# LSTM windows laid out by step, a graph layer in groups of four samples, and a wide layer kept instead of computed twice

## The reference

```python
# L0: eight Euler steps of a graph diffusion (not touched)
# L1: spectral layer, U = eigenvectors of the normalized Laplacian (512x512)
agg = einsum('mn,bnd->bmd', U.T, h);  y = relu(agg @ W1 + b1) @ W2 + b2;  x += einsum('nm,bmd->bnd', U, y)
# L2: A_hat is 512x512, W1 widens 128 to 256, batch statistics over all 8192 rows
a = einsum('nm,bmd->bnd', A_hat, h).reshape(-1, 128)
y = relu(batchnorm(a @ W1.T + b1)) @ W2.T + b2;  x += batchnorm(y)
# L3: two graph convolutions, then for p in 1, 2, 3, 4:
wins = h[:, :nw*p, :].reshape(16*nw, p, 128)      # nw = 512 // p windows of p nodes
last = lstm(Wih[p-1], Whh[p-1], bih[p-1], bhh[p-1], wins)   # p steps, 4 gates
h[:, arange(nw)*p + p-1, :] = last                # written back in place
x += h
```

## Time and profile before

| what | value |
|---|---|
| median of 3 runs | 4364.65 us (4363.6 to 4366.91) |
| profiled execution, its time | 4359.52 us |
| profiled execution, its span | 4357.7 us |
| busy: PE, DVE, ACT, POOL | 2952.5, 2978.4, 982.9, 764.9 us |
| mean granted TensorE clock | 0.818 |

### The profile page before, as it was taken

How to read it: one execution, slowest core, us unless ns; L and a number is a source line. 1 busy time by engine, 2 the same in 40 slices (tenths; PEclk the granted TensorE clock), 3 DMA queues, 4 the chain that set the end, 5 groups by cost and what they waited for, 6 DMA issues and landing times.

```text
span 4357.7 us, 70705 instructions
## 1 busy us (share of the span) xinstructions
PE 2952.5 (68%) x21286; PEld 1968.4 (45%) x21286; DVE 2978.4 (68%) x18190; ACT 982.9 (23%) x3671; POOL 764.9 (18%) x3343
## 2 busy tenths in 40 slices
PE   2899998888888899999710011010064958699998
PEld 1677777777777765555410000000042623354433
DVE  6677888888888868888878889999822122414323
ACT  0222222322322212222210000000013121336532
POOL 0121222222222222333222221111000000000000
PEclk6789999999989959999855555555587979799998
DMA  2000000000000000000000000000000000000000
GB/s 97 2 2 2 2 2 2 2 2 2 2 2 2 2 1 2 2 2 2 1 0 0 0 0 0 0 0 0 0 0 0 0 19 0 0 0 0 1 0 39
DMA packets 3104, 21.16 MB, mean 5 GB/s; under 512 B 432, under 2 KB 560, under 8 KB 1072
## 3 DMA queue, kind: packets, MB, share of 16 engines
q1 hardware_dynamic: 2736, 16.85, 1.0%
HBM read 12.66 MB, written 4.19 MB: 4 GB/s over the span
## 4 chain that ended last, share of the span: by engine, by line
DVE 42%; PE 39%; issue 7%; ACT 6%; POOL 5%; DMA 0%; DVEq 0%; POOLq 0%; ACTq 0%; SPq 0%
PE ps L1023 6%; DVE H L1895 6%; PE ps L710 4%; DVE jq L1469 3%; PE ps L718 3%; POOL step L1077 3%; PE ps L1030 2%; DVE H L1469 2%; POOL C L1078 2%; ACT sz L1290 2%; DVE PQ L1647 2%; PE ps L566 2%; PE ps L660 2%; PE ps L945 2%; DVE SO L1676 1%
## 5 line engine op out<-in xcount | busy, mean ns | idle before, releaser
L718 PE MATMUL ps<-C 128*32 128x131 f32 (+39 forms) x10200 | 379.4, 279 | 16.6 <-DVE C L1664 15.1
L710 PE MATMUL ps<-eye,same 128*128 128x384 f32 x766 | 365.9, 562 | 0.0
L1077 POOL TENSOR_SCALAR step<-XYEG,PQ 128x8 f32<-128x8 f32 (+3 forms) x510 | 158.6, 311 | 1147.7 <-DVE PQ L1647 1147.7
L1290 ACT ACTIVATE sz<-C,PQ 128x4 f32<-128x4 f32 (+3 forms) x510 | 151.6, 297 | 785.0 <-POOL C L1078 785.0
L1023 PE MATMUL ps<-C,V 128*128 128x512 f32 (+1 forms) x504 | 285.9, 724 | 8.4 <-issue 8.4
L718 PEld LDWEIGHTS ps<-C 128*32 128x32 f32 x10200 | 256.6, 115 | 54.5 <-DVE C L1664 20.6
L1274 ACT ACTIVATE tsc<-tsc 128x1 f32<-128x1 f32 x510 | 103.5, 203 | 726.6 <-DVE tsc L1608 726.6
L1469 DVE CUSTOM_DVE_ANT_0 jq<-SO,ps,C 128x10 f32<-128x10 f32 (+14 forms) x1199 | 220.6, 229 | 64.6 <-PE ps L740 12.1
L727 PEld LDWEIGHTS ps<-dots,C 128*128 128x128 f32 x1020 | 172.7, 201 | 182.1 <-DVE dots L1469 94.2
L740 PE MATMUL ps<-C,XYEG 128*128 128x2 f32 (+1 forms) x958 | 186.4, 270 | 101.3 <-POOL C L1078 98.8
L1895 DVE RECIPROCAL H<-H 128x8 f32<-128x8 f32 (+8 forms) x81 | 242.3, 2992 | 2.8
(11 more groups left out here) (515 smaller groups left out, 7414.6 us busy)
## 6 DMA issues: line engine op xcount, KB each, us to landing
out_x<-X SPq DMA_DIRECT2D x4, 1024.0 KB, 3.9
X<-in_x SPq DMA_DIRECT2D x2, 1280.0 KB, 20.3
X<-in_x SPq DMA_DIRECT2D x1, 1536.0 KB, 16.6
eye<-in_eye SPq DMA_DIRECT2D x1, 1026.0 KB, 9.0
WK<-in_adj SPq DMA_DIRECT2D x1, 1024.0 KB, 5.0
adjT<-in_adjT SPq DMA_DIRECT2D x1, 1024.0 KB, 7.0
WK<-in_below SPq DMA_DIRECT2D x1, 1024.0 KB, 11.0
V<-in_wih SPq DMA_DIRECT2D x1, 1024.0 KB, 4.8
```

The lines of the kernel that those rows point to most:

```text
L710: mm(ps[:, 7, 0:n], ident, eye[:, 0, 0:n], start=True, stop=True)
L718: m = mm(ps[q * QUAD:(q + 1) * QUAD, 0, 0:c + n], SI[:, b, 0, 2 * j:2 * j + 1].broadcast_to([P, QUAD]), AS[:, b, q, k * QUAD:P + n], start ...
L1077: step(g_.tensor_scalar(step2[:, k:KB, :], this[:, :, 2:4], PQ[:, r % 2, 1:2], None, ALU.mult))
L1290: fn(sz[:, k:KB].unsqueeze(2), SI[:, k:KB, 0, 2 * j + 1:2 * j + 2], ACT.Copy, scale=PQ[:, r % 2, 2:3])
```

## The change

1. **ln(1) ahead.** DVE takes the statistics of x right after the last merge, before it waits for `gram_ps`; ACT runs `ln_relu` inside the loops that rotate and reflect U, two samples after each copy. The mask `m` moves from TT (in H) to x0T, since H is now written early. `UT` is made after the first two aggregates of L1.
2. **L1 in groups of four.** PE reads H directly, without `stage`. It walks a written-out order; the last product takes four samples at once, 512 columns (`l1_back`). DVE adds it per block of nodes and takes the statistics of ln(2) behind each add.
3. **L2.** The loops are written out. ACT copies the wide layer from PSUM to SBUF (`hidden2`: in Ct and H), DVE takes statistics there, and the second loop starts from the kept values, with W2 alone on PE. ACT runs `ln_relu` of ln(2) inside the first loop. The third loop and the second have four PSUM banks in turn.
4. **LSTM.** For p = 3 and p = 4 GpSimd copies the windows into `SPLIT` (the tiles adjT, ahT, LT, x0T), all inputs of a step side by side. PE's wait for a whole earlier p becomes a wait per samples.
5. **Output.** PE turns Ct directly, with four banks; eight DMAs of two samples.

```diff
+        def hidden2(b, h):
...
+            return (Ct[:, b, :], H[:, b].rearrange("p k d -> p (k d)"))[h]
...
+        SPLIT = [flat_(x) for x in (adjT, ahT, LT, x0T)]
+        def lstm_input(i, s, nbt, p, nw, k):
...
+            if p < 3:
+                return lstm_view((i * 2 + s) * nbt, nbt, p, nw, k)
+            o = s * p * nbt * nw + k * nbt * nw if p == 3 else k * nbt * nw
+            return SPLIT[i if p == 3 else 2 * i + s][:, o:o + nbt * nw]
...
-            for b in range(0, NB, 4):
-                sp.wait_ge(S["out_ready"], b + 4)
...
+            for b in range(0, NB, 2):
+                sp.wait_ge(S["out_ready"], b + 2)
...
+            def l1_back(g):
...
+                pe.wait_ge(S["o_sb"], 4 * g + 4)
+                for nb in range(KB):
+                    n = KB * g + nb
+                    if n > 1:
+                        pe.wait_ge(S["l1_done"], n - 1)
+                    for jb in range(KB):
+                        m = mm(ps[:, 2 + n % 2, :], UT[:, jb, nb * P:(nb + 1) * P], OO[:, :, jb * P:(jb + 1) * P],
+                               start=(jb == 0), stop=(jb == KB - 1))
+                    m.then_inc(S["l1_ps"], 1)
...
             pe.wait_ge(S["back_done"], KB)
+            l1_agg(0)
+            l1_agg(1)
...
-            pe.wait_ge(S["ut_sb"], 1)
...
-            pe.wait_ge(S["ln_out"], NB)
-            with pe.Fori(0, NB // 2) as i:
-                for s in range(2):
...
+            for g in range(NB // 4):
+                b = 4 * g
+                l1_hidden(b)
+                l1_hidden(b + 1)
+                l1_agg(b + 2)
+                if g == 0:
+                    pe.wait_ge(S["ut_sb"], 1)
+                l1_out(b)
+                l1_agg(b + 3)
+                l1_out(b + 1)
+                l1_hidden(b + 2)
+                l1_hidden(b + 3)
+                l1_out(b + 2)
+                l1_out(b + 3)
+                if b + 4 < NB:
+                    l1_agg(b + 4)
+                    l1_agg(b + 5)
+                l1_back(g)
...
-                pe.wait_ge(S["c_y_seen"], 4 * i + 4)
-            with pe.Fori(0, NB // 2) as i:
-                for s in range(2):
-                    for h in range(2):
-                        m = mm(ps[:, 4 * s + h, :], W[("l2W1a", "l2W1b")[h]],
-                               Ct[:, ds(2 * i + s, 1), :].rearrange("p o n -> p (o n)"), start=True, stop=True)
-                    m.then_inc(S["d_y_ps"], 1)
...
+            pe.wait_ge(S["c_y_sb"], 2 * NB)
+            for b in range(NB):
+                pe.wait_ge(S["d_r_sb"], 2 * b + 2)
...
+                    pe.wait_ge(S["d_o_sb"], 2 * (b - 3))
+                for h in range(2):
+                    m = mm(ps[:, 2 * (b % 4), :], W[("l2W2a", "l2W2b")[h]], RL[:, 2 * (b % 2) + h, :], start=(h == 0), stop=(h == 1))
+                m.then_inc(S["d_o_ps"], 1)
...
-                    for s in range(2):
-                        pe.wait_ge(hid_ready[s], base)
...
+                            if k == 0 and p == 2:
+                                for u in range(2):
+                                    pe.wait_ge(hid_ready[u], 2 * i + s + 1)
+                            elif k == 0 and p == 3:
+                                pe.wait_ge(S["split3"], 2 * i + s + 1)
+                            elif k == 0 and p == 4:
+                                pe.wait_ge(S["split4"], 2 * i + s + 1)
...
-                                       lstm_view((i * 2 + s) * nbt, nbt, p, nw, k), start=True, stop=(k == 0))
+                                       lstm_input(i, s, nbt, p, nw, k), start=True, stop=(k == 0))
...
+            for b in range(NB):
+                if b < 2:
+                    pe.wait_ge(gate_sb[b], gates_before(SKIPS + 1))
+                unit, g = divmod(b // 4, 2)
+                if b % 4 == 0:
+                    pe.wait_ge(hid_ready[g], UNITS - SKIPS * (1 - unit))
+                if b > 3:
+                    pe.wait_ge(S["out_ready"], b - 3)
...
-            def stage(staged, used):
...
-                with pool.Fori(0, NB // 2) as i:
-                    for s in range(2):
-                        nc.gpsimd.tensor_copy(HS[:, s, :].rearrange("p (k d) -> p k d", k=KB),
-                                              H[:, ds(i * 2 + s, 1), :, :].rearrange("p o k d -> p (o k) d"))\
...
-            pool.wait_ge(S["ln_out"], NB)
...
-            stage(S["st1"], S["agg_ps"])
...
-            for s in range(2):
-                pool.wait_ge(hid_ready[s], UNITS)
-            with pool.Fori(0, NB // 2) as i:
...
+            for i in range(4):
                 for s in range(2):
...
+                    pool.wait_ge(hid_ready[s], turned2 + 2 * (i + 1))
...
+                    g_.tensor_copy(SPLIT[i][:, s * 6 * n:(s + 1) * 6 * n].rearrange("p (k b w) -> p k b w", k=3, b=2),
+                                   Ct[:, b:b + 2, 0:3 * n].rearrange("p b (w k) -> p k b w", k=3)).then_inc(S["split3"], 1)
+            for i in range(4):
+                for s in range(2):
+                    pool.wait_ge(hid_ready[s], turned3 + 3 * (i + 1))
+                g_.tensor_copy(SPLIT[i].rearrange("p (k b w) -> p k b w", k=4, b=4),
+                               Ct[:, 4 * i:4 * i + 4, :].rearrange("p b (w k) -> p k b w", k=4)).then_inc(S["split4"], 1)
...
+            ln_root(1)
...
+            act.wait_ge(S["ln_in"], 4)
+            for l in range(LOCAL):
...
                 fn(XT_[:, 0:2, :], ps[:, 5:7, :], ACT.Copy).then_inc(S["y_sb"], 1)
+                ln_relu(2 * l)
+                ln_relu(2 * l + 1)
...
-            ln(1)
...
-            ln(2)
...
+                if 2 * LOCAL + n < NB:
+                    ln_relu(2 * LOCAL + n)
...
+            for i in range(NB // 2):
+                for b in range(2 * i, 2 * i + 2):
+                    act.wait_ge(S["c_agg_ps"], b + 1)
+                    fn(AG[:, b % 2, :], ps[:, 4 * (b % 2), :], ACT.Copy).then_inc(S["c_agg_sb"], 1)
+                for b in range(2 * i, 2 * i + 2):
+                    act.wait_ge(S["c_y_ps"], b + 1)
+                    for h in range(2):
+                        fn(hidden2(b, h), ps[:, 4 * (b % 2) + 1 + h, :], ACT.Copy).then_inc(S["c_y_sb"], 1)
+                for b in range(2 * i + 4, min(2 * i + 6, NB)):
+                    ln_relu(b)
...
+            for b in range(NB):
+                if b > 1:
+                    act.wait_ge(S["d_o_ps"], b - 1)
+                for h in range(2):
+                    fn(RL[:, 2 * (b % 2) + h, :], hidden2(b, h), ACT.Relu, bias=bn[:, 8 + h:9 + h], scale=bn[:, 6 + h:7 + h])\
+                        .then_inc(S["d_r_sb"], 1)
...
+            dve.wait_ge(S["x_added"], 4 * KB)
+            ch.restart()
+            ln(1)
...
-            dve.wait_ge(S["x_added"], 4 * KB)
-            ln(1)
...
-            ln(2)
...
+                stats = []
+                for nb in range(KB + 1):
...
+                    if nb < KB:
+                        dve.wait_ge(S["l1_ps"], n + 1)
+                        xb = X[:, 4 * g:4 * g + 4, nb, :]
+                        tt(xb, xb, ps[:, 2 + n % 2, :].rearrange("p (b d) -> p b d", b=4), ALU.add).then_inc(S["l1_done"], 1)
+                    if nb > 0:
+                        dve.wait_ge(S["l1_done"], n)
+                        for b in range(4 * g, 4 * g + 4):
+                            m = ch.mark(v.bn_stats(lnst[:, b * KB + nb - 1, :], X[:, b, nb - 1, :]))
+                        stats.append(m)
+                for b in range(4 * g, 4 * g + 4):
+                    ln_aggr(b, stats[-1])
+            ln_factors(2)
...
-                    tt(xb, xb, ps[:, 4 * (b % 2), :], ALU.add).then_inc(S["e_done"], 1)
+                    tt(xb, xb, ps[:, 2 * (b % 4) + 1, :], ALU.add).then_inc(S["e_done"], 1)
```

More of the change, by code:

```diff
@@ new lines, in _ @@
+            for i in range(NB // 2):
+                two = [(s, 2 * i + s) for s in range(2)]
+                for s, b in two:
+                    pe.wait_ge(S["ln_out"], NB + b + 1)
+                    for nb in range(KB):
+                        m = mm(ps[:, 4 * s, :], H[:, b, nb, :], ahT[:, nb, :], start=(nb == 0), stop=(nb == KB - 1))
+                    m.then_inc(S["c_agg_ps"], 1)
+                for s, b in two:
+                    pe.wait_ge(S["c_agg_sb"], b + 1)
+                    if i > 0:
+                        pe.wait_ge(S["c_y_sb"], 2 * b - 2)
+                    else:
+                        pe.wait_ge(S["l1_done"], NB)
@@ L977, in _ @@
+            pe.wait_ge(S["d_o_sb"], 2 * NB)
+            for b in range(NB):
+                pe.wait_ge(S["e_sb"], b + 1)
+                if b > 3:
+                    pe.wait_ge(S["e_done"], b - 3)
+                for nb in range(KB):
+                    m = turn(ps[:, 2 * (b % 4) + 1, nb * P:(nb + 1) * P], RL[:, b % 4, nb * P:(nb + 1) * P])
+                m.then_inc(S["e_ps"], 1)
+            pe.wait_ge(S["e_done"], NB)
             for i in range(NB // 2):
@@ new lines, in l1_hidden @@
+            def l1_hidden(b):
```

(23 more changed lines are left out.)

180 lines of the change are left out of this document (56 added, 124 removed).

## The result

| | before | changed |
|---|---|---|
| median | 4364.12 us (4358.47 to 4366.91, 4 runs) | 4086.55 us (4062.25 to 4090.32, 4 runs) |
| profiled execution's span | 4357.7 us | 4088.5 us |
| mean granted clock | 0.818 | 0.822 |

The ratio is 0.9354, with a 95% interval of 0.9316 to 0.9391. The forecast was 4092, its range 4065 to 4125.

A forecast was written before the change was run, and what follows sets the result against it. It took TensorE to bound L1's loop and the LSTM, with mostly idle stretches between. Savings of 97.2 + 64.7 + 4.4 + 89.0 + 16.1 = 271.4 us gave 4088 profiled, 4092 forecast; range 4065 to 4125 (8 in 10).

The forecast's parts named there:

- B: L2's first two loops with statistics: from 194.2 us to 129.5, 64.7 us saved.
- A: L1 with ln(1) ahead and the gap to L2: from 252.9 us to 155.7, 97.2 us saved.
- C: L2's third loop, 37.31 us: four banks gain between 0 and 8.0 us, 4.4 taken.
- E: Output, 34.3 us: no staging and early turns leave 18.2 us, some 16 us saved.
- The reason for L1's waits: L1's loop: TensorE stood 1.36 us for DVE's add and between the small products for ScalarE.
- D: LSTM: waits 7.3, records 29.3 and 56.4, less 4 for GpSimd's copies, 89.0 us saved.
- The lock (1): LSTM: GpSimd's copies and DVE's two-input operations exclude each other, at worst 18 us, 14 more than priced; chance 0.10.
- The second loop (2): L2's second loop runs at half clock throughout, 27 us more, whole time 4119 us; chance 0.08.
- ln(1) (3): Ahead of L1: DVE's work for ln(1) is not hidden, 19.4 us more, 4111 us; chance 0.04.
- The stride rival (4): LSTM: strided reads aren't what costs, or the copies' reader is as slow; 85.7 us less saved, 4178 us; chance 0.03.
- The clock (5): Dense stretches from L1 on: granted clock falls to 1.2 GHz and stays, slower than before, 4790 us if throughout; chance 0.01.

The follow-up runs named there:

- the plain order: Changed kernel with TensorE's L1 program in plain order (aggregates, W1 twice, W2 twice, again, then the product with U): 4068.06 us, one run; L1's loop 148.7 us.
- e4: Changed kernel with the four long copies for p = 4 made by ScalarE in place of GpSimd: 4080.35 us median, ratio to before 0.9346.
- e1: Changed kernel reading strided views of Ct at p = 3 and 4, without GpSimd copies: 4166.13 us median, ratio to before 0.9541.
- e2: Changed kernel without copies, p = 3 and 4 reading nodes side by side from Ct (computes something else): 4066.94 us median of 2 runs.

## Why the prediction was right, point by point

**The terms.** The sum of 271.4 us met 269.2, and no term missed by more than 4.4. That it met so closely is in part luck: the five priced stretches saved 276.5 us, 5.1 more than the sum, and three stretches priced at nothing gave back 7.4, of which 3.1 are in the eigenvalue part, whose length differs by tens of us between executions (last section). B was 129.5 as foretold, in all four parts: 85.6, 7.1, 31.5, 5.3 for 85.7, 7.4, 30.9, 5.5. In A ln(1) went under as priced (5.60 left, 5.3 foretold); the gap was 7.92 for 7.2. The loop with its turn of U took 143.4, not 148.5. Of the 5.1 a pair's price was 2.9: it came from before's rows as 17.7 and was 17.3, since by starts W1 took 1.71 or 1.80 for 1.81, W2 1.78 or 1.89 for 1.94, and the product with U and the aggregates 6.87 for 6.97. The turn of U was 1.7 at full clock and not 3. And of "I leave 4 us for four groups' ends and a cold start" 3.0 came: the cold start was 1.8 us, seen at the first aggregates (8.83 for 7.03), and only the last group's end cost something, 1.2.

Two sums of the prediction don't come out, without harm. "Half" of C's 0 to 8.0 is 4.0 and not 4.4 (5.2 came; no run says by what). And in A's parts nothing accounts for the 1.1 in "50.03 − 3.0 − 1.1": 47.0, 37.7 and 12.5 make the 97.2. E was 17.9 for 16.1: the sixteen adds ran in a row of 9.63 us, 0.60 each, where the prediction had 0.69.

**The reason for L1's waits** was named wrongly in part. The prediction had TensorE stand for ScalarE between the small products; before's trace lists no such wait, and the plain order shows it once. What it stood for is DVE: 0.78 us at each group's end in the plain order, and in before the 1.34 to 1.37 ahead of each turn but the first.

**D** was 87.1 for 89.0. The waits gave more than 7.3: 6.4 in the stretch of p = 1 and 2, and 119.15 − 115.81 = 3.3 at p = 3, 9.7 in all; the prediction took the 2.44 us ahead of p = 4 three times, and before's trace lists 3.09 ahead of p = 2 and 2.88 ahead of p = 3. The term that was mis-sized is the lock, 7.4 by e4 for 4. The prediction had the copy at 2.45 to 5.06 us and stalls of 0.9 to 3.5 each; the copy took 3.88 and three stalls 2.2. I priced it as if the copies might fall between DVE's operations. They can't here: both wait for the end of a group's last cell, which DVE itself computes. It releases the copy, and DVE goes on to the next group's first cell update, whose gates ScalarE has ready 0.17 us later. So the copy starts just when that update is due.

**The rivals.** The lock (1) came at two fifths of its upper price, 7.4 of 18. The second loop (2) ran at clock 0.92: 0.66 in its first 7.8 us and 1.00 behind them. ln(1) (3) was hidden. The stride rival (4) fell by e1 and e2: at stride 3 the stretch takes 115.81 us against 87.07 and at stride 4 149.37 against 92.87, for matmuls that read float32. The Trainium skill ("SBUF — State Buffer", section "Door 1: The DMA port swizzle") says that one can stride for free up to four fp32; these runs contradict it for TensorE's input. The clock (5) stood at 0.97 to 1.00 in L1, in L2's first loop and in the LSTM.

**What beats both.** e4_act: the same kernel with the long copies on ScalarE. In the trace it is 7.4 us shorter at p = 3. The medians (4080.35 against 4086.55) point the same way, but the changed kernel's own runs lie 28 us apart, so the whole times alone don't show it.

## What to carry to other kernels

Price a strided operand by one row with the stride and one without, from the same kernel. Where both exist, what the stride costs can be foretold to a microsecond (29.3 and 56.4 for 28.7 and 56.5 here). What the copy that avoids it costs was less sure: 7.4 us, where 4 had been priced. When a helper copy goes to GpSimd, ask which event releases it, and which two-input DVE operation comes due at that moment; if it is the critical one, try the copy on ScalarE (7.4 us here). A normalization in front of a loop falls into three parts that can move apart: statistics behind the adds that make the data (14 us here), the factors, and the relus, of which only the first few samples' must come before the first matmul (23 us here, with the staging copy).
